# A block-wise attention in four engine queues: eight steps of one batch's preparation and finish are put at other units

## The reference

```python
x = x + _L0_attn_a_ref(_layernorm(x, axis=-1), L0_attn_a_W)
# in _L0_attn_a_ref, 16 heads of 8 features:
qkvgr = jnp.einsum('btc,oc->bto', x, W)
log_g = jax.nn.log_sigmoid(qkvgr[..., 3 * C:])
log_G = jnp.cumsum(log_g, axis=1).transpose(0, 2, 1)
S = jnp.einsum('bhtd,bhsd->bhts', Q, K)
Tm = DEG * jnp.log(jnp.abs(S) + EPS) + jnp.log(jnp.float32(scale))
Z = Tm + log_G[..., :, None] - log_G[..., None, :]
Z = jnp.where(mask, Z, -jnp.inf)            # causal
P = jnp.exp(Z - Z_rowmax)
y = jnp.einsum('bhts,bhsd->bhtd', P, V) / jnp.sum(P, axis=-1)[..., None]
```

## Time and profile before

| | us |
|---|---|
| median of 3 runs | 1274.48 |
| lowest, highest | 1269.55, 1278.74 |
| the profiled execution | 1268.58 |
| its span in the trace | 1266.2 |
| PE busy in the span | 893.8 (71%) |
| DVE, ACT, POOL busy | 732.7, 533.1, 531.9 |
| mean granted clock of PE | 0.80 |

### The profile page before, as it was taken

The page is one execution under the profiler, slowest core; times in us unless marked ns, Lnnn a source line. Parts: engine busy times, 40 slices in busy tenths (PEclk is TensorE's granted clock), DMA queues, the critical chain, the costliest instruction groups (busy, mean ns, idle before and its releaser), DMA issues. The chain is left out here.

```text
span 1266.2 us, 25954 instructions
## 1 busy us (share of the span) xinstructions
PE 893.8 (71%) x9215; PEld 617.4 (49%) x9215; DVE 732.7 (58%) x1572; ACT 533.1 (42%) x1192; POOL 531.9 (42%) x603
## 2 busy tenths in 40 slices
PE   3788979789797842099919598948767783407993
PEld 2355455454554521088804278516555572106882
DVE  6556575565745673012263189999999999401223
ACT  4557566575665611044506420035555540104441
POOL 3454446544455313634430000037777760272442
PEclk8678697786977856599969799978798886758996
DMA  6132141230412050266633910000002100016675
GB/s 186 54 115 100 43 142 52 92 126 17 142 50 94 3 202 23 63 191 198 181 88 135 260 38 1 1 0 1 0 0 66 33 25 9 13 52 174 201 199 162
DMA packets 134915, 111.75 MB, mean 88 GB/s; under 512 B 27248, under 2 KB 120368, under 8 KB 134384
## 3 DMA queue, kind: packets, MB, share of 16 engines
q1 hardware_dynamic: 129264, 99.66, 26.4%
q0 software_dynamic: 5120, 10.53, 2.4%
q10 hardware_dynamic: 432, 0.20, 0.1%
HBM read 64.80 MB, written 45.43 MB: 87 GB/s over the span
## 5 line engine op out<-in xcount | busy, mean ns | idle before, releaser
L663 DVE TENSOR_SCALAR a_mag<-a_pS 128x1024 int32<-128x1024 int32 (+1 forms) x192 | 176.4, 945 | 80.5 <-PE a_pS L867 69.5
L440 ACT ACTIVATE a_pw<-a_mag,a_eps_a 128x1024 f32<-128x1024 f32 (+1 forms) x192 | 170.0, 927 | 51.5 <-DVE a_mag L663 49.9
L325 POOL TENSOR_TENSOR a_pw<-a_pw,a_decay 128x256 f32<-128x256 f32 x128 | 96.1, 752 | 201.1 <-ACT a_pw L440 200.8
L1161 POOL DMA_INDIRECT ys_dram<-f_yo,f_who x96 | 92.0, 958 | 127.4 <-DVE f_yo L1361 110.7
L867 PE MATMUL a_pS<-a_qf,a_kf 64*64 64x192 bf16 (+3 forms) x1536 | 119.2, 285 | 19.3 <-DVE a_mag L663 17.7
L1349 DVE TENSOR_SCALAR f_ysT<-f_bY,f_b2s 128x256 f32<-128x256 f32 x48 | 23.2, 483 | 175.7 <-PE f_bY L1449 174.4
L1708 POOL TENSOR_TENSOR d_pb_p<-d_Q,d_s_sb 128x512 f32<-128x512 f32 x32 | 37.4, 1168 | 195.6 <-ACT d_s_sb L1808 195.6
L1204 ACT ACTIVATE f_hs<-f_bH,f_b1s 128x256 f32<-128x256 f32 x192 | 75.4, 475 | 65.6 <-PE f_bH L1439 65.5
L2181 PE MATMUL d_c<-d_pb_p,d_ident 128*128 128x256 f32 x256 | 73.1, 456 | 42.1 <-POOL d_pb_p L1714 42.1
L1153 POOL DMA_INDIRECT xs_dram<-f_xa,f_pos x64 | 61.6, 962 | 92.8 <-DVE f_pos L1334 73.9
L899 PE MATMUL a_pOff<-a_pw,a_vo 128*18 128x64 f32 x3584 | 97.7, 245 | 0.0
(11 more groups left out here) (348 smaller groups left out, 1785.1 us busy)
## 6 DMA issues: line engine op xcount, KB each, us to landing
parts_scratch<-a_parts SPq DMA_DIRECT2D x32, 384.0 KB, 3.3
f_w1s<-in_L_ffn_w_dram SPq DMA_DIRECT2D x48, 256.0 KB
f_w2s<-in_L_ffn_w_dram SPq DMA_DIRECT2D x48, 256.0 KB
a_kf<-parts_scratch SPq DMA_DIRECT2D x16, 512.0 KB, 4.9
a_qf<-parts_scratch SPq DMA_DIRECT2D x16, 512.0 KB, 6.2
xs_dram<-blank SPq DMA_DIRECT2D x12, 516.0 KB, 5.2
f_xs<-xs_dram SPq DMA_DIRECT2D x48, 129.0 KB, 2.3
parts_scratch<-a_parts SPq DMA_DIRECT2D x16, 256.0 KB, 2.5
```

Of the source, the lines that this page charges most:

```text
L325: pool.tensor_tensor(own, own, decay[:, k, m, hf:NP:2, :], ALU.mult)\
L440: act.activation(pw[:, n % 4, 0:N], mag[:, n % 3, 0:N], ACT.Square, bias=eps_a[:, 0:1])\
L663: dve.tensor_scalar(mag[:, n % 3, 0:2 * N].bitcast(I32).rearrange("p (l t) -> p l t", l=2), pS[:, 2 * (n % 2):2 * (n % 2) + 2, 0:N].bitcas ...
L1161: pool.indirect_dma_start(ys_dram[f][:, :], bass.IndirectOffsetOnAxis(ap=who[:, q, a:a + 1], axis=0), yo[:, q, a, :], None).then_inc(ys_ou ...
```

## The change

Eight moves, and nothing that is added or taken away:

- `gate_log` on POOL from unit 14, where it stood behind `diagonal(14)`, to unit 13, which has no diagonal block.
- `values` on ACT: the first half at unit 12 and the second at 13, where both stood at 13 ahead of `square(14)`.
- PE's `sums` at unit 15 behind `attend(14)`; they stood ahead of it.
- DVE's `sums` at unit 16, behind `magnitude(18)`, with `cum_split`; they stood behind `magnitude(17)`.
- `token_decay` on ACT at unit 18, behind `square(18)`; it stood behind `square(17)`. Its wait is now for the second instruction of `cum_split` instead of the third.
- `reach_sums` and `reach_bound` at unit 18, and `reaches` at unit 20: one unit later each.
- FIN[0] from 18 to 19: `turn_back` and `finish` of the even half a unit later, and `add_half` at 21 instead of 20. At both finishes parts 0 and 1 now stand behind the magnitude of their own unit, where they stood ahead of it.
- `values_off` one unit later each, from unit 21 on.

```diff
-        FIN = (18, 2)
+        FIN = (19, 2)
...
-            return [j for j in range(NM - 1) if j == n - SUMS - 5]
+            return [j for j in range(NM - 1) if j == n - SUMS - 6]
...
-                    if n == VALUES + 5:
+                    if n == VALUES + 4:
                         gate_log(b + 1)
...
-                act.wait_ge(s["cum_split"], 4 * bb + 3)
+                act.wait_ge(s["cum_split"], 4 * bb + 2)
...
+                    if n == VALUES + 3:
+                        values(b + 1, 1 - k, 0)
                     if n == VALUES + 4:
                         gate_logs(b + 1)
-                    if n == VALUES + 4:
-                        values(b + 1, 1 - k, 0)
                         values(b + 1, 1 - k, 1)
-                    if n == SUMS + 2:
+                    if n == SUMS + 3:
                         token_decay(b + 1, 1 - k)
-                    if n == SUMS + 4:
+                    if n == SUMS + 5:
                         reaches(b + 1)
...
+                    if n + 2 < NU:
+                        magnitude(b, n + 2)
+                    elif not last:
+                        magnitude(b + 1, n + 2 - NU)
                     if n == FIN[0]:
                         finish(b, k, 0, 0)
                         finish(b, k, 0, 1)
...
-                    if n + 2 < NU:
-                        magnitude(b, n + 2)
-                    elif not last:
-                        magnitude(b + 1, n + 2 - NU)
...
-                    if n == SUMS:
+                    if n == SUMS + 1:
                         sums(b + 1)
-                    if n == SUMS + 1:
                         cum_split(b + 1)
-                    if n == SUMS + 2:
+                    if n == SUMS + 3:
                         reach_sums(b + 1)
                         reach_bound(b + 1)
...
-                    if n == SUMS and not last:
-                        sums(b + 1)
                     if n >= 1:
                         attend(b, k, n - 1)
                     elif not first:
                         attend(b - 1, 1 - k, NU - 1)
+                    if n == SUMS and not last:
+                        sums(b + 1)
```

## The result

The changed kernel took 1222.49 us in the median of 4 runs (1216.11 to 1228.95), the kernel before 1273.12 beside it: a ratio of 0.9599, 95% interval 0.9536 to 0.9661. The gain is 51 us where 22 were worked out.

The account below looks back on a forecast made before the run. DVE bounds units 18 to 21, PE at half clock from unit 22 on; seven batches give 18.9 us, the seventh 1.5 more, the last 1.5: 22 us off 1268.58, so 1246.6, 1252 as a median; range 1237 to 1268.

Parts of the forecast that it names:

- the rival of the clock: PE's clock stays up, unit 22 on runs faster: 8 us for one unit per batch, 17 for two; 1244 to 1235; chance 0.2.
- Units 12 to 16: ACT, POOL, PE: earlier `square(14)` and `gate_log` bring scores(18) 1.2 us earlier; PE waits 1.6 instead of 2.8 us.
- Units 16 to 22: DVE's reordered row starts scores(24) 2.1 us earlier, other end 2.7, taken as 2.3; PE waits twice for magnitudes, about 1 each.
- Units 2 to 4: `magnitude(4)` runs inside DVE's 3.51 us wait for turned-back sums: 0.4 us per batch, 0.5 at unit 20 of the last.
- the `issue` wait: Sign in the profile: DVE's `issue` wait at L687 is down by a third.
- SP's round trip: SP's copies and read of `there`, behind `cum_split`, just fit before the decay sums; any gain past 2.2 needs `cum_split` earlier.
- The 7.1 us behind `cum_split`: Time from the end of `cum_split` to the decay sums when SP's trip decides; used in the slower rival, chance 0.04.
- POOL: `diagonal(21)` now ahead of `values_off`, which hid at half clock: 1.5 us once, seventh batch, and 1 for the last.
- the sum: 7 x (2.3 + 0.4) = 18.9, the seventh batch 1.5, the last one 1.5: 22 us gained.
- The last batch: Gain of 1.5 us: 1 from POOL's order and 0.5 from the finish at unit 20.

Follow-up runs that it names:

- run 10: Kernel before, with `values_off` and the even `add_half` one unit later on POOL, and zero-adding products filling PE's waits at units 15, 20, 21: 1229.3 us, 0.9576.
- run 3: Changed kernel with PE's sums at unit 15 ahead of `attend(14)` again: 1233.3 us, 0.9621 of the kernel before.
- run 12: Changed kernel once more with no edit, on another chip: 1240.6 us, 0.9658 of the kernel before.
- run 8: Kernel before with POOL's order alone changed, `values_off` and the even `add_half` one unit later, no fillers: 1278.2 us, 0.9966.
- run 9: Kernel before with zero-adding filler products in PE's waits (36 at unit 15, 22 at 20, 9 at 21), POOL's order left: 1263.0 us, 0.9844.
- run 1: Kernel before with fewer zero-adding filler products in PE's waits (18 at unit 15, 10 at 20, 4 at 21): 1278.7 us, 0.9948.
- run 4: Changed kernel with the finish one unit earlier and ahead of its unit's magnitude again (FIN = (18, 2)): 1271.7 us, 0.9908 of the kernel before.
- run 5: Changed kernel with zero-adding filler products in PE's four waits (18, 18, 11, 7): 1216.1 us, 0.9471 of the kernel before.
- run 6: Changed kernel with fillers in PE's waits and PE's sums ahead of `attend(14)`, 7 fillers behind them: 1210.3 us, 0.9432 of the kernel before.

## Why the prediction was wrong

- **The step that failed** is the rival of the clock, and in it two things. The reasoning: "PE is 12.17 of 12.20 busy in that stretch and still is not granted more, so the decay sums look like work that doesn't hold the clock." They hold it: 0.39 us each from 128.27 on, and all through run 10. The row said only that a clock which had fallen did not come back during them in that batch. I read a failure to rise as a failure to hold; and even the rise isn't shut out, since the first batch of the changed kernel has it at 88.47. The earlier trace rows had scores of unit 24 at full clock and I used them for a price, not as evidence. And the size: I priced one or two units at 1.2 us. When the clock holds, the whole stretch from scores(24) to unit 0 goes from 11.2 to 7.0 us, and the way to unit 12 from 21.7 to 19.5: 6.5 us, over five units' worth. Seven batches of that would be 45 us; five kept the clock, 32.5. With the chance of 0.2 and the price of 8 to 17 us, neither the forecast nor the range could reach it.
- **Units 12 to 16**: as worked out. The wait for the logarithm is gone and `attend(14)` waits 1.56 us for diagonal(14), where 1.6 was forecast. Not foreseen: that the sums' 0.95 us behind `attend(14)` is time lost (run 3), since they would fit into this wait.
- **Units 16 to 22**: unit 12 to scores(24) is 2.69 us shorter; I gave 2.1 and 2.7 as ends and took 2.3. The upper end holds, with its reason (units 15 to 18 at full clock), which means that a part of it was already the clock's. magnitude(20) stands ahead of the reach. PE waits three times for magnitudes, 1.55, 0.93 and 0.67, where I had two of about 1.
- **Units 2 to 4**: the `issue` wait is gone wholly, not by a third, but the 0.4 us aren't seen in the length: in the batch where the clock fell, unit 0 to unit 12 takes 21.77, before 21.62. PE's idle time in it did go from 1.39 to 1.02 us, as forecast; it was busy 0.5 longer, at a clock of 0.86 instead of 0.89.
- **SP's round trip** just fits, as forecast: no wait in the first trace of the changed kernel, one of 0.83 us in run 12, and 0.26 in run 3, which comes a microsecond sooner. The 7.1 us behind `cum_split` were near: the decay sums start 6.4 behind it without a wait (121.88 to 128.27), and where they waited in run 3 they started 6.7 to 7.6 behind it.
- **POOL**: "With PE at half clock it hid" is right, and run 8 shows it: 0.3%. That it hid only there is the same step again. The full clock makes POOL's queue a wait of 1.5 us in each batch (run 9), and that wait takes the clock away. I counted it once, for the seventh batch.
- **Had the clock behaved as I took it**, 7 times 2.6 and the last batch's 1.8 give 20 us, against the 22 of the sum: the working of the waits was sound.
- **The last batch** gained 1.8 us (15.9 to 14.1), forecast 1.5.

The Trainium skill ("TensorE: Matmul & The Clock Gate", Part 1) says that activity releases the throttle and idleness brings it back. The second half agrees with the trace: the falls looked at here stand in or within about a microsecond behind such waits. The first doesn't always: PE was busy 11.19 of 11.19 us at 0.50, but in the first batch the clock came back at 88.5 us out of a PE as busy. That contradiction is what I built on, and it didn't bear the weight. The same page says of the rise at a kernel's start that "it's run-variable". Here the fall varies too: waits of 1.55, 0.93 and 0.67 us left the clock up in one batch, and 1.55, 0.82 and 0.66 didn't in another.

## What to carry to other kernels

Where a row shows the granted clock at half, don't ask first whether the work in that stretch could hold it, but what waits stood just ahead of the fall, and price the whole stretch until it comes back at the full clock's durations of the same instructions; moves that save two microseconds of waits there can be worth nine. Ask also what is hidden only because the engine is slow: another engine's queue that costs nothing at the low clock can be the wait that brings it down again. Filler products in PE's waits can tell what the clock is worth, if there are enough of them and no wait is left open: in run 1 there were too few, and in run 9 POOL's queue took the clock away all the same. In a kernel that lies on the edge they may stay: they made this one faster and its runs more alike.

## What the runs showed of the hardware

- The clock, once down, mostly stayed at 0.50 through 11 us and more of a PE without gaps (decay sums of 512 columns, with scores and value products between), and came back in the products behind unit 0. In three batches it came back within that stretch: in the changed kernel at 88.5 us, in run 3 at 185.5, in run 4 at 87.0. Once up, it stayed up through the same instructions, unless a wait came. Why this mix holds the full clock and seldom brings it back isn't settled: no run changed the products themselves.
- It fell after waits of 1.5 to 2.8 us on PE, and in some batches after three of 1.6, 0.8 and 0.7 us within 7 us. The longest wait doesn't decide: in run 1 it fell behind waits of 1.05 and 0.47 us (339 to 342 us) and held behind 1.40 and 0.47 (391 to 394).
- Products that add zeros hold the clock as others do: 0.99 from 46 to 358 us in runs 5, 6 and 10.
- In run 4 the five periods behind the first were equal to 0.1 us (51.2), with the fall at the same place of each; in runs 9 and 10 they were as equal (51.1 and 44.5), in the others they vary by 1 to 7 us but for a batch or two. That the waits and the clock's changes lock to each other is a guess; nothing here tests it.
